# Attention scores from rounded halves of q and k, two heads stacked in one pass, in an eight-block kernel on one core

## The reference, cut to what matters

```python
x = L0_attn_x                                        # 4 x 1024 x 512, fp32
x = x + _layernorm(_L0_attn_ref(_layernorm(x, axis=-1), ...), axis=-1)
x = x + _layernorm(_L0_ffn_ref(_layernorm(x, axis=-1), ...), axis=-1)
```

```python
def step(S, inp):
    qb, kb, vb = inp
    inter = jnp.einsum('bhcd,bhde->bhce', qb * decay_q[None, :, :, None], S)
    scores = jnp.einsum('bhcd,bhed->bhce', qb, kb) * dmask[None]
    intra = jnp.einsum('bhce,bhed->bhcd', scores, vb)
    S_new = lam_c[None, :, None, None] * S + jnp.einsum('bhcd,bhce->bhde', kb * decay_k[None, :, :, None], vb)
    return (S_new, inter + intra)
```

## Time and profile before

| what | value |
|---|---|
| median of 3 runs | 2029.71 us (2024.03 to 2031.78) |
| the profiled execution, its own time | 2037.38 us |
| its span in the trace | 2035.3 us |
| granted TensorE clock, mean | 0.982 |
| busy: TensorE, weight loads, DVE, ACT, GpSimd | 94%, 76%, 60%, 47%, 21% |

### The profile page before, as it was taken

How to read it: one execution, slowest core, us unless ns; L and a number is a source line. 1 busy time by engine, 2 the same in 40 slices (tenths; PEclk the granted TensorE clock), 3 DMA queues, 4 the chain that set the end, 5 groups by cost and what they waited for, 6 DMA issues and landing times.

```text
span 2035.3 us, 27981 instructions
## 1 busy us (share of the span) xinstructions
PE 1903.8 (94%) x9880; PEld 1538.7 (76%) x9880; DVE 1213.9 (60%) x2890; ACT 951.3 (47%) x1916; POOL 437.5 (21%) x438
## 2 busy tenths in 40 slices
PE   6789999999989999999999999999899999999996
PEld 5566777677766777777777767778898988989875
DVE  4556665574664574575475566564566666666576
ACT  4344444343443443444354344333566666666553
POOL 2301001001001001100100100120455555555322
PEclk9889999999999999999999999999999999999998
DMA  7976246336245328326436434555688989988597
GB/s 280 370 259 215 66 146 225 122 115 228 90 160 200 112 93 271 133 83 220 145 125 207 138 103 156 167 223 165 182 251 252 256 252 260 255 252 250 136 274 184
DMA packets 137705, 387.67 MB, mean 190 GB/s; under 512 B 16848, under 2 KB 16992, under 8 KB 130656
## 3 DMA queue, kind: packets, MB, share of 16 engines
q0 software_dynamic: 49584, 203.33, 33.4%
q1 hardware_dynamic: 87552, 182.49, 27.4%
q10 hardware_dynamic: 432, 0.07, 0.0%
HBM read 281.08 MB, written 104.74 MB: 190 GB/s over the span
## 4 chain that ended last, share of the span: by engine, by line
PE 73%; DVE 11%; DMA 8%; ACT 4%; issue 3%; POOL 1%; SPq 1%; DVEq 0%; ACTq 0%; POOLq 0%
PE banks L749 20%; PE banks L751 19%; PE banks L750 19%; DMA moe_dn_raw<-w_dn,w_index 5%; PE banks L816 4%; PE banks L830 2%; PE banks L836 2%; PE banks L823 1%; DMA xT_lo<-xt_scratch 1%; DVE pair_stats L1143 1%; PE banks L782 1%; PE banks L937 1%; DVE probsT L1300 1%; PE banks L943 1%; PE banks L812 1%
## 5 line engine op out<-in xcount | busy, mean ns | idle before, releaser
L749 PE MATMUL banks<-xT_hi,ffn_gate_up_hi 128*128 128x512 f32 x704 | 298.9, 425 | 8.3 <-DMA xT_lo<-xt_scratch 6.4
L751 PE MATMUL banks<-xT_hi,ffn_gate_up_lo 128*128 128x512 f32 x704 | 277.7, 394 | 0.0
L750 PE MATMUL banks<-xT_lo,ffn_gate_up_hi 128*128 128x512 f32 x704 | 277.3, 394 | 0.0
L749 PE MATMUL banks<-moe_gu_hi,moe_xT_hi 128*128 128x352 f32 x568 | 197.1, 347 | 5.7 <-DVE moe_xT_lo L1455 5.7
L1015 ACT COPY q_one_head<-qT 32x128 f32<-32x128 f32 x512 | 151.1, 295 | 94.5 <-PE banks L816 89.2
L1448 DVE TENSOR_TENSOR moe_gu_lo<-moe_gu_raw,moe_gu_hi 128x704 fp32r<-128x704 f32 x156 | 135.8, 887 | 87.5 <-ACT moe_gu_hi L1072 81.6
L751 PE MATMUL banks<-moe_gu_hi,moe_xT_lo 128*128 128x352 f32 x568 | 183.8, 324 | 0.0
L750 PE MATMUL banks<-moe_gu_lo,moe_xT_hi 128*128 128x352 f32 x568 | 183.0, 322 | 0.0
L749 PEld LDWEIGHTS banks<-xT_hi,ffn_gate_up_hi 128*128 128x128 f32 x704 | 133.9, 190 | 52.3 <-issue 12.7
L750 PEld LDWEIGHTS banks<-xT_lo,ffn_gate_up_hi 128*128 128x128 f32 x704 | 134.1, 190 | 33.9 <-issue 9.1
L751 PEld LDWEIGHTS banks<-xT_hi,ffn_gate_up_lo 128*128 128x128 f32 x704 | 133.7, 190 | 29.1
(11 more groups left out here) (298 smaller groups left out, 4373.3 us busy)
## 6 DMA issues: line engine op xcount, KB each, us to landing
ffn_w_raw<-w_ffn SPq DMA_DIRECT2D x176, 384.0 KB
att_w_hi<-att_w_split SPq DMA_DIRECT2D x112, 256.0 KB, 3.7
att_w_lo<-att_w_split SPq DMA_DIRECT2D x112, 256.0 KB, 4.3
x_normed_by_expert<-x_normed POOLq DMA_DIRECT2D x26, 771.0 KB, 16.4
x_in<-x SPq DMA_DIRECT2D x32, 256.0 KB, 4.4
x<-x SPq DMA_DIRECT2D x32, 256.0 KB, 5.3
out<-x POOLq DMA_DIRECT2D x32, 256.0 KB, 2.6
fin_ffn_out<-ffn_out SPq DMA_DIRECT2D x32, 256.0 KB, 7.5
```

The costliest lines, as they stand in the source:

```text
L749: pe.matmul(out_ap, l_hi, r_hi, start=start, stop=False)
L750: pe.matmul(out_ap, l_hi, r_lo, start=False, stop=False)
L751: return pe.matmul(out_ap, l_lo, r_hi, start=False, stop=stop)
```

## The change

Scores are now made of rounded halves, too. Names: `QH`, `KH` (ACT) round q and k of two groups to fp32r, `QL`, `KL` (DVE) subtract to get the low halves. `q_hi_and_lo` holds, for each pair of heads of a group, the 64 rows of the high half and, on the other 64 partitions, the same rows of the low half. `k_hi_twice` holds k's high half of that pair on both halves of the partitions, `k_lo_one_pair` its low half on the pair's own 64 partitions and zeros elsewhere. `Z` multiplies all 128 partitions with a scale per partition (`head_of_pair`, 1 for the rows of head `j` of a pair and 0 for the rest) where it copied 32 rows four times. `S` then takes four fp32r matmuls of 256 columns: for each pair of heads, k's high half against the stack of q's high and low half, and k's low half against the same columns. That is the sum of the same three products as elsewhere.

Beside that: `k_decayed` takes its decay from a table of 16 columns spread by the access pattern, where it was a table of 512 columns; `state_new` shares the buffer of `k_decayed`, for which `KT` waits on the `ST` before it; `PASSES` counts 2 for an `S` where it counted 4; and nearly all pieces of an attention block have new places. The diff, cut to its core (of the tables of places three lines are shown):

```diff
--- before.py
+++ after.py
-    "S": (19, 20, 22.82, 23.75, 27.39, 27.94, 30.85, 30.94, 35.49, 36.49, 38.49, 39.49, 43.69, 44.69, 46.69, 47.69,),
+    "KH": (16.9, 19.2, 22.78, 26.88, 30.7, 34.8, 38.32, 42.42,),
+    "KL": (17.5, 20.2, 23.78, 27.88, 31.7, 35.8, 39.32, 43.42,),
+    "S": (18.5, 19, 22.2, 22.7, 26.18, 26.68, 29.88, 30.38, 34.1, 34.6, 37.8, 38.3, 41.72, 42.22, 45.42, 45.92,),
...
-PASSES = {"T1": 2, "QK": 12, "V": 12, "KT": 2, "S": 4, "IP": 6, "ST": 4, "OUT": 12, "T2": 2, "R1": 12, "R2": 2, "RK": 1,
+PASSES = {"T1": 2, "QK": 12, "V": 12, "KT": 2, "S": 2, "IP": 6, "ST": 4, "OUT": 12, "T2": 2, "R1": 12, "R2": 2, "RK": 1,
...
-        qz = sb("q_one_head", [2, GH, P], scope=phase1)
+        pair_of = sb("head_of_pair", [2], scope=phase1)
+        q2 = sb("q_hi_and_lo", [2, 2, P], F32R, scope=phase1)
+        qz = sb("q_one_head", [2, GH, P], F32R, scope=phase1)
+        k2 = sb("k_hi_twice", [2, 2, P], F32R, scope=phase1)
+        kl = sb("k_lo_one_pair", [2, 2, P], F32R, scope=phase1)
         qd = sb("q_decayed", [G, P], scope=phase1)
         kd = sb("k_decayed", [D], scope=phase1)
         probs = sb("probsT", [2, GH, P], scope=phase1)
         state = sb("state", [G, P], scope=phase1)
-        state_new = sb("state_new", [G, P], scope=phase1)
+        state_new = kd[:, :].rearrange("p (g d) -> p g d", d=P)
...
+        def z_count(a, c, g):
+            return NC * G * a + G * c + g + 1
+
+        def s_before(a, c, g):
+
+            n = z_count(a, c, g) - 3
+            return n // (NC * G), n // G % NC, n % G
...
+                pe.wait_ge(v_piece, done("V", "KL", a, c, g // 2))
                 pe.wait_ge(a_piece, done("A", "Z", a, c, g))
-                mm = pe.matmul(b, kT[:, g, c * P:(c + 1) * P], qz[:, g % 2].rearrange("p h t -> p (h t)"),
-                               start=True, stop=True)
+                for i in range(2):
+                    cols = slice(2 * i * P, 2 * (i + 1) * P)
+                    q_pair = qz[:, g % 2, 2 * i:2 * i + 2].rearrange("p h t -> p (h t)")
+                    pe.matmul(b[:, cols], k2[:, i, g % 2, :], q_pair, start=True, stop=False)
+                    mm = pe.matmul(b[:, cols], kl[:, i, g % 2, :], q_pair, start=False, stop=True)
...
+            elif kind == "QH":
+                c, half = args
+                if (c, half) == (0, 0):
+                    act.wait_ge(a_piece, done("A", "QK", a, G - 1))
+                n = 2 * NC * a + 2 * c + half - 1
+                if n >= 0:
+                    act.wait_ge(a_piece, done("A", "Z", n // (2 * NC), n // 2 % NC, n % 2 * 2 + 1))
+                for i in range(2):
+                    r = slice(2 * i * HD, 2 * (i + 1) * HD)
+                    op = act.copy(q2[r, i, :, :], qT[r, 2 * half:2 * half + 2, c * P:(c + 1) * P])
+            elif kind == "KH":
+                c, half = args
+                if (c, half) == (0, 0):
+                    act.wait_ge(a_piece, done("A", "QK", a, 2 * G - 1))
+                n = 2 * NC * a + 2 * c + half - 1
+                if n >= 0:
+                    act.wait_ge(p_piece, done("P", "S", n // (2 * NC), n // 2 % NC, n % 2 * 2 + 1))
+                for i in range(2):
+                    r = slice(2 * i * HD, 2 * (i + 1) * HD)
+                    for to in (r, slice(2 * HD - r.start, 4 * HD - r.start)):
+                        op = act.copy(k2[to, i, :, :], kT[r, 2 * half:2 * half + 2, c * P:(c + 1) * P])
             elif kind == "Z":
                 c, g = args
-                if (c, g) == (0, 0):
-                    act.wait_ge(a_piece, done("A", "QK", a, G - 1))
-                if 4 * c + g >= 2:
-                    act.wait_ge(p_piece, done("P", "S", a, *divmod(4 * c + g - 2, G)))
-                for j in range(GH):
-                    r = slice(j * HD, (j + 1) * HD)
-                    op = act.copy(qz[r, g % 2, j, :], qT[r, g, c * P:(c + 1) * P])
+                act.wait_ge(v_piece, done("V", "QL", a, c, g // 2))
+                if z_count(a, c, g) == 1:
+                    act.wait_ge(const_v, 8)
+                if z_count(a, c, g) > 2:
+                    act.wait_ge(p_piece, done("P", "S", *s_before(a, c, g)))
+                for j in range(2):
+                    op = act.activation(qz[:, g % 2, j::2, :], q2[:, :, g % 2, :].bitcast(F32), ACT.Copy, scale=pair_of[:, j:j + 1])
...
+                if NC * a + c:
+                    ve.wait_ge(v_piece, done("V", "ST", *divmod(NC * a + c - 1, NC)))
                 ve.tensor_tensor(qd[:, :, :], qT[:, :, c * P:(c + 1) * P], dq[:, :, :], ALU.mult)
-                op = ve.tensor_tensor(kd[:, :], b, dk[:, :], ALU.mult)
+                op = ve.tensor_tensor(kd[:, :].rearrange("p (h d) -> p h d", d=HD), b.rearrange("p (h d) -> p h d", d=HD),
+                                      dk[:, :].unsqueeze(2).to_broadcast([P, HEADS, HD]), ALU.mult)
+            elif kind == "QL":
+                c, half = args
+                ve.wait_ge(a_piece, done("A", "QH", a, c, half))
+                for i in range(2):
+                    r, to = slice(2 * i * HD, 2 * (i + 1) * HD), slice(2 * (1 - i) * HD, 2 * (2 - i) * HD)
+                    op = ve.tensor_tensor(q2[to, i, :, :], qT[r, 2 * half:2 * half + 2, c * P:(c + 1) * P],
+                                          q2[r, i, :, :].bitcast(F32), ALU.subtract)
+            elif kind == "KL":
+                c, half = args
+                ve.wait_ge(a_piece, done("A", "KH", a, c, half))
+                for i in range(2):
+                    r = slice(2 * i * HD, 2 * (i + 1) * HD)
+                    op = ve.tensor_tensor(kl[r, i, :, :], kT[r, 2 * half:2 * half + 2, c * P:(c + 1) * P],
+                                          k2[r, i, :, :].bitcast(F32), ALU.subtract)
...
-            ve.memset(qz[:, :, :, :], 0.0).then_inc(const_v, 1)
+            ve.memset(kl[:, :, :, :].bitcast(F32), 0.0).then_inc(const_v, 1)
...
+                    heads = blk[:, :].rearrange("p (h d) -> p h d", d=HD)
+                    ve.tensor_tensor(pair_of[:, :], heads[:, 0:2, 0], heads[:, 2:4, 0], ALU.add).then_inc(const_v, 1)
-    dk = np.exp(-slope[head][None, :] * (P - 1 - pos)[:, None])
+    dk = np.exp(-slope[None, :] * (P - 1 - pos)[:, None])
```

More of the change, by code:

```diff
@@ L94 @@
     "L": (38.45, 53.52,),
-    "LX": (39.49, 54.8,),
+    "LX": (39.8, 54.8,),
     "x1o": (39.67, 41.23, 52.1, 54.3,),
-    "T2": (41.6, 42.6, 56, 56.74,),
-    "xto": (58.7,),
+    "T2": (41.6, 43.33, 56, 56.74,),
+    "xto": (58.73,),
     "R1": (58,),
@@ L101 @@
     "SM1": (59.42,),
-    "SM2": (60.46,),
+    "SM2": (60.77,),
     "SM3": (61.11,),
-    "SM4": (62.49,),
+    "SM4": (61.31,),
     "CM": (62.12,),
-    "RK": (64.43,),
-    "sc": (59.36,),
+    "RK": (64.1,),
+    "sc": (63.19,),
     "PG": (66.47,),
@@ L119 @@
     "N1": (2.61, 3.16, 4.61, 5.61,),
[8 rows of a table removed]
-    "OUT": (28.27, 35.39, 44.8, 50.87,),
[12 rows of a table added]
+    "OUT": (28.27, 35.12, 44.8, 50.87,),
+    "xr": (24.94, 25.24, 45.39, 45.61,),
+    "LO": (36.6, 51,),
+    "LN": (37.86, 53.51,),
+    "L": (38.45, 53.1,),
+    "LX": (39.49, 54.8,),
+    "x1o": (39.42, 41.23, 52.1, 56.27,),
+    "T2": (41.6, 42.6, 56, 56.74,),
+    "R1": (58,),
+    "R2": (59.41,),
+    "SM1": (59.42,),
+    "SM2": (59.89,),
+    "SM3": (61.11,),
+    "SM4": (62.49,),
+    "CM": (62.83,),
+    "RK": (64.21,),
+    "sc": (66.53,),
+    "PG": (66.44,),
 }
-ARGS = {"Z": (NC, G), "S": (NC, G), "IP": (NC, 2)}
+ARGS = {"Z": (NC, G), "QH": (NC, 2), "QL": (NC, 2), "KH": (NC, 2), "KL": (NC, 2), "S": (NC, G), "IP": (NC, 2)}
 def attention_offsets(a):
@@ L432, in build @@
         dq = sb("decay_q", [G, P], scope=phase1)
-        dk = sb("decay_k", [D], scope=phase1)
+        dk = sb("decay_k", [HEADS], scope=phase1)
         lam = sb("state_decay", [G], scope=phase1)
@@ L1492, in build @@
         block = ctx.enter_context(nc.Block())
-        ATT = ("N1A", "N1B", "N1", "W", "T1", "QK", "V", "KT", "Z", "S", "IP", "ST", "OUT", "LO", "LN", "L", "LX", "T2", "R1", "R2",
+        ATT = ("N1A", "N1B", "N1", "W", "T1", "QK", "V", "KT", "QH", "QL", "KH", "KL", "Z", "S", "IP", "ST", "OUT", "LO", "LN", "L", "LX", "T2", "R1", "R2",
                "SM1", "SM2", "SM3", "SM4", "CM", "RK", "PG")
@@ L1525, in _ @@
                 if p == ("R1", 0):
-                    pe.wait_ge(const_v, 8)
+                    pe.wait_ge(const_v, 9)
                     pe.wait_ge(const_a, 1)
@@ L1565, in _ @@
                 ve.memset(t[:, :], 0.0).then_inc(const_v, 1)
-            late = next(p for p in ORDER["V"] if p[0] in ("V", "KT"))
+            late = next(p for p in ORDER["V"] if p[0] in ("V", "KT", "Z", "QL"))
             for p in ORDER["V"]:
```

15 lines of the change are left out of this document (3 added, 12 removed), and 33 rows, old and new, of tables (OPENING, PLACES).

## The result

The changed kernel is slower: 2108.64 us median (2105.15 to 2110.92, four runs) against 2029.88 us (2024.03 to 2031.78, four runs), a ratio of 1.0385 with a 95% interval from 1.0367 to 1.0404. The forecast was 1994 us.

The account below looks back on a forecast made before the run. TensorE's work was taken to bound the kernel from 200 us on. Scores -41.7 and -2.0, block 0 +4, waits +4 gave -36 us, from the 2029.7 us median to 1994 us; eight-in-ten range 1980 to 2013.

Parts of the forecast that it names:

- The score matmuls: Each S in the attention blocks: 0.47 us instead of 0.86, saving 0.39; bounds 0.44 and 0.64 us an S.
- The added instructions: Per S on ACT and DVE: Z 0.50 us, QH and KH 402 ns each, QL and KL 419 ns each.
- In this stage time taken from TensorE comes off the end, as long as DVE and ACT keep up: From 200 to 1300 us: TensorE, busy 1053.8 of 1100 us, sets the pace, so its savings shorten the kernel.
- The term of 41.7 + 2.0 us: Saving from shorter scores: 41.7 us for 107 S after 200 us, 2.0 for the five S before.
- I take 4 us, with 0 and 20 as the bounds: After 200 us: growth of TensorE's waits from added DVE and ACT load, 4 us, between 0 and 20.
- The share of 70% for DVE and 54% for ACT: Steady attention stage: busy shares with the added work, up from 59% and 42%, said to leave both engines room.
- Block 0: First attention block: ends 4 us late from added work on the path, bounds 0 and 10 us.
- the 3.2 us: Block 0, chunks after the first: six of twelve S each save 0.54 us, 3.2 us set against the delays.
- The rival of the late k: Half-to-half hand-over: single k buffers make KH and the next S wait, 1.2 us at each place, 2059 us; chance 0.03.
- waits eat the gain: DVE and ACT hold TensorE up in new places: 20 us of waits gives 2010 us, 30 gives 2020; chance 0.14.
- All cases that end slower: Whole kernel: late k (0.03, 2059 us) and weight loads in the open (0.01, 2081 us); chance 0.04.
- The sign that I announced: Profile after: prediction wrong if waits for probsT, attT_lo or hidden_lo exceed 40 us, or first scores repeatedly await `k_lo_one_pair`.

Follow-up runs that it names:

- the matmuls alone: Kernel before, with S replaced by four fp32r matmuls of 256 columns on fixed zeros, ACT and DVE work unchanged: 2017.20 us, ratio 0.9947.
- the full set of pieces at the old places: Changed kernel with the attention pieces of blocks 1 to 7 back where they stood before, new ones put between: 2102.13 us, ratio 1.0359.

## Why the prediction was wrong

**The score matmuls: right.** 0.48 us an S for 0.47 forecast. The lower bound was read from the wrong kind of row: the eight records of 128 columns at 0.11 us are the state's update, four fp32 matmuls in two records each, and say nothing of fp32r; the rows of 512 and 352 columns carried the forecast. The Trainium skill, "TensorE: Matmul & The Clock Gate", Part 3, "The mechanism", has the sentence that a load overlaps running matmuls only when the row groups differ, which would have made each of the four a load plus a matmul; the same section also lets a load into a background weight buffer go ahead of them. A step of 0.12 us with a load record of 200 ns in it disagrees with the first and shows again that full-height loads run beneath the matmuls before them.

**The added instructions: right.** Z took 498 ns for 500, QL and KL 420 and 414 for 419, QH and KH 403 and 404 for 402. ACT got 111.5 us more work over the span and DVE 97.3.

**"In this stage time taken from TensorE comes off the end, as long as DVE and ACT keep up": this step failed.** I read it from a busy share of 96% and short waits. The term of 41.7 + 2.0 us came to 11 for all 128 S: with DVE and ACT untouched, 49 us less gave 11, and 61 us put back on cost 14. TensorE's records overlap (0.39 us long at a step of 0.23), so its busy share says how tightly the stage is packed, not that the engine alone sets its pace. A shorter S makes TensorE wait for the same partners a little longer (for probsT 15.2 us in 8 waits where it was 11.0 in 8, from 200 to 1290 us) and lowers its clock; in blocks 2 to 6 these two took 7 and about 8 of 30 us.

**"I take 4 us, with 0 and 20 as the bounds" for new waits: this failed with it, and is the larger part.** In blocks 2 to 6 alone TensorE's idle time grew by 44 us, and over the whole kernel the added pieces cost 84 us at the old places. The share of 70% for DVE and 54% for ACT was taken as room. The table prices it: of 84 us between the matmuls alone and the full set of pieces at the old places, 54 come with the added work itself, which by shares should have been free, and 30 with the waits that tie the pieces together. Per microsecond of work, length on DVE cost 0.34 (22 us for 107 less 41), on ACT 0.23 (31 us for 133 more: 113.5 less 60.3 for Z, 51.6 less 24.9 for QH, 103 less 50 for KH); at 8 us either way the two prices don't differ for certain. At these prices no single engine is the bound and each is a part of it: the change earned 0.22 times 49 and was charged for some 220 us of other work (372 us in the groups of the added instructions, less the 151.1 of the copies removed).

**The clock wasn't in the sum.** It was at 1.00 from 200 us on the earlier trace rows, and I counted waits by their length, so a term was put at nothing. The stretch at 394 us shows a wait of 2 us with the lower level right behind it. In blocks 2 to 6 this is 17 of the 61 us that go against the gain.

**Block 0: 15 us late, not 4.** Its timeline:

```profile
51.54 0.55 PE L857 MATMUL banks<-q_one_head,k_hi_twice 128*128 128x256 f32 x1 [6.81 <-ACT q_one_head L1077]
53.57 0.77 PE L786 MATMUL banks<-att_w_hi,x_normedT_hi 128*128 128x512 f32 x1
72.95 0.75 PE L864 MATMUL banks<-q_decayed,state 128*128 128x128 f32 x4 [3.37 <-DVE probsT L1379]
144.90 0.77 PE L786 MATMUL banks<-x_normedT_hi,att_w_hi 128*128 128x512 f32 x1 [3.50 <-DVE x_normedT_lo L1341]
```

The first V was forecast for 52.7 and came at 53.57; the second IP for 70.1 and came at 72.95. The rest was missed: TensorE waits 23.9 us for probsT in this block where it waited 15.8, and the clock from 60 us to the block's end is 0.78 instead of 0.86. I let six of twelve S save 0.54 us in a stretch that DVE paces, and counted five pairs of its subtractions. The matmuls alone, with DVE's work as before, saved nothing in this block (132.3 us against 129.8), so the 3.2 us had no ground.

**The rival of the late k** named the right mechanism at the wrong size. Most of its waits on ACT lie beside work of TensorE; taking them away gave 16 us. It was a part, not the cause. The rival "waits eat the gain" was the right one, stopped too early at 30 us: nothing in the profile gave that bound. All cases that end slower had 0.04 between them.

**The sign that I announced didn't show.** TensorE's waits for probsT, attT_lo and hidden_lo sum to 15.6 us from 200 to 1300 us, not over 40, and the first score of a half waits for `k_lo_one_pair` only once, 2.0 us in block 0: the waits changed their partners (state, att_w_lo, x_normed). What did show was the busy share, 90% for TensorE where over 94 was forecast (995 of 1100 us), with DVE at 64% and ACT at 49% where 70 and 54 were: the stage got longer, not fuller. A forecast of waits should name their sum, or TensorE's idle time, and not their kinds.

**The new places** weren't priced at all. With the old pieces they cost 117 us, and with the new ones they are no better than the old places (5 us, give or take 6). Whether some other set of places does better stays open; moving the pieces at the three worst stalls gave 6 us, and even with all added work gone the old order left 11 us of gain.
